# One attention stage, its work put in another order on three engines, and two tiles cut to their natural size

## What is computed

```python
Q = normalize((x @ W_q.T)); K = normalize((x @ W_k.T)); V = x @ W_v.T      # per head
Qn = normalize(einsum('bthd,hde->bthe', Q, W_nudge))
scores = einsum('bqhd,bkhd->bhqk', Qn, K) * SCALE
s = sigmoid(3.0 * einsum('bthd,rd->bthr', K, simple_roots))
cw = prod(s[..., None, :] * bits + (1 - s[..., None, :]) * (1 - bits), -1)  # 16 weights
scores += einsum('bthc,hc->bth', cw, chamber_bonus) of the key             # then causal mask
out = (softmax(scores) @ V).reshape(b, t, 1024) @ W_out.T
```

## Time and profile before

| | |
|---|---|
| median of 3 runs | 1827.04 us (1826.31 to 1828.17) |
| profiled execution, its own time | 1828.17 us |
| span of that execution, first to last instruction | 1826.4 us |
| mean granted TensorE clock | 0.969 of full speed |
| TensorE matmul busy | 1664.5 us, 91% of the span |
| VectorE busy | 1356.9 us, 74% |
| GpSimd busy | 990.9 us, 54% |
| ScalarE busy | 890.1 us, 49% |
| attention layer | from the start to about 833 us |

### The profile page before, as it was taken

One profiled execution on the slowest core, in us unless ns is written; L12 is line 12 of the kernel. 1 busy time (PEld: TensorE's weight loads), 2 busy tenths in 40 slices (PEclk: granted clock), 3 DMA queues, 4 the chain that ended last, 5 costly groups with the idle time before them and its releaser, 6 DMA issues.

```text
span 1826.4 us, 43279 instructions
## 1 busy us (share of the span) xinstructions
PE 1664.5 (91%) x12768; PEld 1245.9 (68%) x12768; DVE 1356.9 (74%) x4113; ACT 890.1 (49%) x2003; POOL 990.9 (54%) x1779
## 2 busy tenths in 40 slices
PE   3999999999999999975999999999999998669996
PEld 2676666676776666754778888888888886435553
DVE  6788888888888887764466777777777775648886
ACT  2665656665556665532444444444444443224443
POOL 5777777777777777752222333333333333227777
PEclk8999999999999999997999999999999999579998
DMA  1011111111111111201011000000000002434441
GB/s 41 10 38 42 52 52 52 52 52 52 44 34 52 52 52 52 81 13 41 12 58 58 30 30 30 30 29 29 29 29 29 29 24 88 155 105 134 130 134 44
DMA packets 78239, 95.76 MB, mean 52 GB/s; under 512 B 7046, under 2 KB 62995, under 8 KB 78160
## 3 DMA queue, kind: packets, MB, share of 16 engines
q1 hardware_dynamic: 70992, 77.91, 13.6%
q0 software_dynamic: 7168, 16.87, 2.6%
HBM read 53.14 MB, written 43.69 MB: 53 GB/s over the span
## 4 chain that ended last, share of the span: by engine, by line
PE 46%; DVE 3%; issue 2%; POOL 2%; ACT 1%; DMA 0%; DVEq 0%; POOLq 0%; SPq 0%; ACTq 0%
PE main L1243 7%; PE main L1245 6%; PE main L1252 6%; PE main L1431 4%; PE main L1269 3%; PE yp L1402 3%; PE xi L1219 3%; PE main L1386 2%; PE main L1389 2%; PE main L1387 2%; PE main L1290 2%; PE route L1445 1%; PE turn L1212 1%; PE xi L1445 1%; PE yp L1453 1%
## 5 line engine op out<-in xcount | busy, mean ns | idle before, releaser
L653 ACT ACTIVATE wgu<-score 128x384 f32<-128x384 f32 x512 | 223.2, 489 | 103.1 <-PE score L476 101.7
L498 PE MATMUL outp<-wgu 128*64 128x256 f32 (+1 forms) x2048 | 197.9, 336 | 29.8 <-POOL wgu L321 28.7
L321 POOL TENSOR_SCALAR_AFFINE_SELECT wgu<-wgu 128x512 f32<-128x512 f32 x256 | 167.1, 653 | 104.4 <-ACT wgu L653 92.1
L1243 PE MATMUL main<-hT_high,h_high 128*128 128x512 f32 x512 | 221.2, 432 | 0.9 <-ACT hT_high L1503 0.9
L1245 PE MATMUL main<-hT_high,h_low 128*128 128x512 f32 x512 | 201.3, 393 | 0.0
L498 PEld LDWEIGHTS outp<-wgu 128*64 128x64 f32 x2048 | 129.4, 138 | 89.5 <-issue 36.4
L1252 PE MATMUL main<-hT_low,h_high 128*128 128x512 f32 x512 | 138.4, 391 | 0.1
L792 DVE TENSOR_TENSOR wgu<-spread,wgu 128x512 f32<-128x512 f32 x128 | 88.5, 691 | 61.0 <-PE spread L520 46.3
L1843 DVE SCALAR_TENSOR_TENSOR th<-th,main 128x512 f32<-128x512 f32 x64 | 43.9, 686 | 114.0 <-ACT th L1570 114.0
L534 PE MATMUL back<-wout,wgu 128*128 128x128 f32 x1024 | 128.1, 279 | 0.0
L1219 PEld LDWEIGHTS xi<-state,wh_sb 128*128 128x128 f32 x512 | 93.8, 196 | 41.0 <-ACT state L1480 23.9
(11 more groups left out here) (272 smaller groups left out, 4299.7 us busy)
## 6 DMA issues: line engine op xcount, KB each, us to landing
sorted_d<-row_buf SPq DMA_DIRECT2D x26, 772.0 KB, 3.7
xg<-sorted_d SPq DMA_DIRECT2D x48, 386.0 KB, 3.1
wgu<-in_gate_up SPq DMA_DIRECT2D x4, 2048.0 KB, 9.4
xa<-in_x SPq DMA_DIRECT2D x32, 128.0 KB, 3.5
xr<-in_x SPq DMA_DIRECT2D x32, 128.0 KB, 3.2
x_d<-x SPq DMA_DIRECT2D x32, 128.0 KB, 1.9
x1c<-x_d SPq DMA_DIRECT2D x16, 256.0 KB, 2.8
x1v<-x_d SPq DMA_DIRECT2D x16, 256.0 KB, 2.8
```

The costliest lines, as they stand in the source:

```text
L321: pool.affine_select(out=blocks, in_=blocks, compare_op=ALU.is_ge, fill=0.0, base=0, pattern=[[0, 4], [1, P]], channel_multiplier=-1).then ...
L498: m = pe.matmul(outp[DV * i:DV * (i + 1), p % 2, k * P:T], val[par][:, k, h, :], weights(h, k), start=(k == 0), stop=(k == 1), tile_positi ...
L653: act.activation(prob[:, h // 2 % (RING // 2), :, h % 2, :], score[h % BANKS][:, 0:SC].rearrange("p (c q) -> p c q", q=P), ACT.Exp).then_i ...
L1243: pe.matmul(main[m % 2][:, :], w[0][:, k, m * P:(m + 1) * P], src[0][:, k, :], start=(k == 0), stop=False)
```

## The change

Three things. (1) `k5` and `cmax` get their natural size: the bonus matmul loads 16 weight columns instead of 128, the `cmax` matmul contracts over 16 rows instead of 128, and two memsets go (N_CONST from 19 to 17). (2) In TensorE's step the pieces stand in another order: the turning of xn comes right behind the first `scores` and ahead of `weighted(z, 3)`; `values` 1, 2 and 3 come earlier, values 3 right behind the bonus; `spread_out(z, 1)` comes ahead of `scores` 4 and `spread_out(z, 2)` ahead of `scores` 5; `scores` 6 comes right behind the `cmax` matmul, with the keys turned behind it; the wait for `rec` is moved ahead of the `outp` matmuls of group 0. (3) ScalarE's and VectorE's steps are put in the matching order. GpSimd's step keeps its order, and so does SyncE's.

```diff
-        k5_wide = sb("k5", [P, P + HEADS, DH + 1])
-        k5 = k5_wide[:, 0:TT * HEADS, :].rearrange("p (i h) c -> p i h c", i=TT)
+        k5 = sb("k5", [P, TT, HEADS, DH + 1])
-        cmax = sb("cmax", [P, T])
+        cmax = sb("cmax", [HEADS, T])
-        N_CONST = 19
+        N_CONST = 17
-                const(pool.memset(k5_wide[:], 0.0))
-                const(pool.memset(cmax[:], 0.0))
@@ weighted, TensorE
                 if g == 0:
                     wait(pe, s["val"], 4 * (b + 1))
+                    wait(pe, s["rec"], b)
...
-                if g == 0:
-                    wait(pe, s["rec"], b)
@@ step, TensorE: the new order
                 scores(b, par, 0)
                 (wait xn, wait qraw; turn xn into front)      # was behind scores 1
                 weighted(z, 1 - par, 3)
                 scores(b, par, 1)
                 values(f, par, 0)
                 (wait xnT; Q and K projection)
                 values(f, par, 1)                             # was behind scores 3
                 scores(b, par, 2)
                 weighted(b, par, 0)
                 spread_out(z, 0)                              # was behind values 1
                 scores(b, par, 3)
                 values(f, par, 2)                             # was behind the bonus
                 (wait bon; turn the bonus, 16 weight columns)
                 values(f, par, 3)                             # was behind the turned qkn
                 spread_out(z, 1)                              # was behind scores 5
                 scores(b, par, 4)
                 weighted(b, par, 1)
                 spread_out(z, 2)                              # was behind the cmax matmul
                 scores(b, par, 5)
                 (wait qkn; turn qkn)
                 (wait cmax; cmax matmul, 16 rows)
                 scores(b, par, 6)                             # was behind the turned keys
                 (wait q5; turn k_aug)                         # was behind the rotation
                 (wait qkT; rotation)
                 spread_out(z, 3)                              # was behind scores 7
                 weighted(b, par, 2)
                 scores(b, par, 7)
                 output(z, par, range(0, 5))
@@ step, ScalarE: moved
+                xnT ahead of copy_out(z, 1 - par, 3)          # was behind weights 2, 3
+                copy_values(f, par, 1) behind sq1             # was behind weights 6, 7
+                copy_values(f, par, 3) behind copy_values 2   # was behind qkT
@@ step, VectorE: moved
+                normalise(z, par, 2) ahead of q5              # was behind q5
+                normalise(z, par, 3) behind k_augT            # was behind the sigmoid and ssg2
```

More of the change, by code:

```diff
@@ L324, in split @@
             def split(value, part, name, n):
-                v = value.rearrange("p i h c -> p (i h c)")
+                v = value[:].rearrange("p i h c -> p (i h c)")
                 parts = [part[:, k].rearrange("p r c -> p (r c)") for k in range(3)]
@@ L437, in step @@
                     wait_apart(pool, s["p_qaT"], f, s["const"])
-                    split(q5[:], q_part, "qsplit", f)
+                    split(q5, q_part, "qsplit", f)
                 mask(b, 6)
@@ L564, in step @@
                 scores(b, par, 0)
-                weighted(z, 1 - par, 3)
-                scores(b, par, 1)
                 if n is not None:
@@ L573, in step @@
                     mm.then_inc(s["p_xnT"], 1)
+                weighted(z, 1 - par, 3)
                 if isinstance(f, int) and f == 0:
@@ L577, in step @@
                     pe.wait_ge(s["wv_split"], 2)
+                scores(b, par, 1)
                 values(f, par, 0)
@@ L586, in step @@
                     mm.then_inc(s["p_qk"], 1)
+                values(f, par, 1)
                 scores(b, par, 2)
                 weighted(b, par, 0)
+                spread_out(z, 0)
                 scores(b, par, 3)
-                values(f, par, 1)
-                spread_out(z, 0)
+                values(f, par, 2)
                 if f is not None:
@@ L597, in step @@
                     for i in range(TT):
-                        mm = pe.matmul(turned[:, i * P:(i + 1) * P], k5_wide[:, i * HEADS:i * HEADS + P, DH], ident[:],
+                        mm = pe.matmul(turned[0:HEADS, i * P:(i + 1) * P], k5[:, i, :, DH], ident[:],
                                        start=True, stop=True)
                     mm.then_inc(s["p_bonT"], 1)
-                values(f, par, 2)
+                values(f, par, 3)
+                spread_out(z, 1)
                 scores(b, par, 4)
                 weighted(b, par, 1)
+                spread_out(z, 2)
                 scores(b, par, 5)
-                spread_out(z, 1)
                 if n is not None:
@@ L618, in step @@
                         mm = pe.matmul(turned[:, T + i * HEADS:T + (i + 1) * HEADS], cmax[:, i * P:(i + 1) * P],
-                                       ident[:, 0:HEADS], start=True, stop=True)
+                                       ident[0:HEADS, 0:HEADS], start=True, stop=True)
                     mm.then_inc(s["p_cmax"], 1)
-                spread_out(z, 2)
+                scores(b, par, 6)
+                if f is not None:
+                    wait(pe, s["q5"], f + 1)
+                    turn_operands(k_aug, "k", f)
                 if n is not None:
@@ L627, in step @@
                     mm.then_inc(s["p_rot"], 1)
[L628 to L632, removed]
+                spread_out(z, 3)
                 weighted(b, par, 2)
                 scores(b, par, 7)
-                spread_out(z, 3)
                 output(z, par, range(0, 5))
@@ L682, in step @@
                     act.activation(xnT[par][:], front[:, 0:T], ACT.Copy).then_inc(s["xnT"], 1)
+                copy_out(z, 1 - par, 3)
+                weights(b, 2, 3)
                 copy_values(f, par, 0)
@@ L688, in step @@
                                    ACT.Square).then_inc(s["sq1"], 1)
+                copy_values(f, par, 1)
                 weights(b, 4, 5)
@@ L695, in step @@
                 weights(b, 6, 7)
-                copy_values(f, par, 1)
                 copy_values(f, par, 2)
+                copy_values(f, par, 3)
                 weights(b, 8, 9)
@@ L840, in step @@
                     wait(dve, s["p_cmax"], f)
-                    dve.tensor_tensor_scan(out=cmax[0:HEADS, :], data0=bonT[:], data1=bonT[:], initial=bonT[:, 0:1],
+                    dve.tensor_tensor_scan(out=cmax[:], data0=bonT[:], data1=bonT[:], initial=bonT[:, 0:1],
                                            op0=ALU.max, op1=ALU.max).then_inc(s["cmax"], 1)
@@ L845, in step @@
                     split_weight(3)
+                normalise(z, par, 2)
+                if last:
                     split_weight(4)
@@ L850, in step @@
                                       -1.0, None, ALU.mult).then_inc(s["q5"], 1)
-                normalise(z, par, 2)
                 if y is not None:
@@ L867, in step @@
                        .then_inc(s["kaT"], 1)
+                normalise(z, par, 3)
                 if last:
@@ L880, in step @@
                     dve.wait_ge(s["ssg2"], n + 1)
-                normalise(z, par, 3)
                 if y is not None:
```

6 lines of the change are left out of this document (1 added, 5 removed).

## The result

| | before | after |
|---|---|---|
| median | 1827.26 us (4 runs, 1826.31 to 1828.17) | 1858.83 us (4 runs, 1858.22 to 1860.25) |
| profiled execution, its own time | 1828.17 us | 1857.88 us |
| span of that execution | 1826.4 us | 1856.1 us |
| mean granted clock | 0.969 | 0.967 |

The ratio is 1.0175, with a 95% interval of 1.0158 to 1.0191: the kernel became slower by 31.6 us. Predicted were 1853 us, between 1826 and 1868.

A forecast was written before the change was run, and what follows sets the result against it. TensorE (91% busy), waiting for GpSimd's mask 3, was taken as the bound. The new loop summed to 25.26 us a step against 24.28: 27 x 0.98 less 1 on 1828.17 gives 1853.7, 1853 for the median; range 1826 to 1868.

The forecast's parts named there:

- The step that decides: Loop from one end of xn to the next through TensorE, GpSimd and VectorE: 25.26 us a step against 24.28.
- X: The moment VectorE finishes xn of the next element, from which the prediction counts the loop.
- X to `spread_out(z, 1)`: From the end of xn to that spread's start, by TensorE's work or VectorE's run to `normalise` 0: 11.12 us average.
- to the end of `scores` 5: TensorE from `spread_out(z, 1)` over `scores` 4, `weighted(b, 1)` and `spread_out(z, 2)` to `scores` 5's end: 3.64 us.
- to mask 5: From the end of `scores` 5 on TensorE to mask 5 on GpSimd: 1.11 us.
- mask 5 to rstd, the wait for q5 gone: GpSimd's stretch from mask 5 to rstd: 7.26 us with a 0.59 wait for q5, 6.67 without it.
- rstd to X: VectorE's yn, x1 and xn behind rstd: 2.72 us.
- wait at xn: TensorE stands for xn of the next element behind `scores` 0, some 0.8 us in every step.
- L520 waits for L792: TensorE's `spread_out(z, 1)` waits for VectorE's `normalise` 0 in every other step of the loop.
- The narrow tiles: Bonus and `cmax` matmuls on TensorE: costed at nothing in the loop; bonus worth up to 0.56 us a step uncovered.
- The wait for `rec`: TensorE's wait at `weighted(b, 0)`: costs nothing, reciprocal ready about 5.2 us after X, matmul starts at 5.5.
- The clock: Rival: TensorE's waits drop its clock once a step, 11 to 32 us on top; 0.11, shared with a longer chain.

The follow-up runs named there:

- e1: Kernel before, with only `spread_out` 1 moved ahead of `scores` 4 and `spread_out` 2 ahead of `scores` 5: 1911.73 us, ratio 1.0461.
- e3: Kernel after, with xn's turning and ScalarE's xnT put back where they were: 1854.98 us, ratio 1.0151.
- e4: Kernel after, with `spread_out` 1 and 2 put back and VectorE's `normalise` 2 behind `q5` again; xn stays early: 1845.52 us, ratio 1.0104.
- e6: Kernel after, with xn's turning, xnT, `spread_out` 1 and 2 and `normalise` 2 all put back: 1838.73 us, ratio 1.0069.
- e7: Kernel before, with GpSimd's mask 3 moved right behind mask 2, ahead of the split of k: 1799.82 us, ratio 0.985.
- e9: Kernel after, with the wide `k5` and the 128-row `cmax` back: 1856.42 us, ratio 1.0162.
- e5: Kernel before, with only `k5` and `cmax` in natural size and the two memsets gone: 1834.71 us, ratio 1.0045.
- e12: Kernel after, with xn's turning and xnT back and the wait for `rec` back between the `outp` and `total` parts: 1868.60 us, ratio 1.0221.
- e8: Kernel after, with GpSimd's mask 3 moved right behind mask 2: 1857.12 us, ratio 1.0168.

## Why the prediction was right, and where it was off

**The step that decides, right.** The loop from xn over `spread_out(z, 1)`, mask 5 and rstd sets the step. Summed: 25.26 us; measured: 25.23 in the step shown, 25.20 on average. e1 shows that asking early for the spreads is enough to close it, without any wait for xn; e3 shows that removing the visible wait of 0.87 us gives 0.07 us a step. e4 and e6 show that undoing parts of the change makes it shorter (24.72 and 24.41) and doesn't open it: in e4 TensorE still waits for xn in each step, in e6 for the reciprocal behind it. In the kernel before it isn't this loop that sets the step but the wait for mask 3, as e7 shows.

**Its terms.**

| term | predicted | measured |
|---|---|---|
| X to `spread_out(z, 1)` | 11.12: TensorE 10.9, VectorE 11.35 in every other step | 11.13 or 11.20, by TensorE in all steps but one |
| to the end of `scores` 5 | 3.64 | 3.54 |
| to mask 5 | 1.11 | 1.10 |
| mask 5 to rstd, the wait for q5 gone | 6.67 | 6.67 |
| rstd to X | 2.72 | 2.72 |
| wait at xn | 0.8 | 0.87 |

The first term is right by two errors, which is luck. VectorE's run was 10.76 us on average and not 11.02, so it didn't decide. TensorE was 0.30 later than summed in the step shown: 0.17 since xn turned takes 0.36 and not 0.19 ahead of `outp`, 0.08 since it starts 0.13 and not 0.05 behind X. V takes 0.89 and 0.90 and not 0.80 ahead of `scores` and the bonus, but the sum had most of that in its 0.37 for `scores` and in the wait ahead of V 3. That L520 waits for L792 in every other step was wrong, then; it did so once. The count of changes of shape was off too: the step has 24 where the prediction counted 22, and 27 with the two narrow pieces.

**The narrow tiles, right where they stand and wrong as a rule.** They cost nothing in the new order (e9). But "the `cmax` matmul still loads 128 columns: nothing" was wrong: it costs 0.28 us a step where TensorE's path is open (e5), by its changes of shape and not by its columns. The bonus matmul saves 0.26 us and not up to 0.56, and 0.10 of that goes again. (No row stood behind the prediction's 0.25 us for it; it takes 0.55.)

**The wait for `rec`, right by a narrow margin.** The reciprocal ends 5.11 to 5.18 us after X, as said, and `weighted(b, 0)` starts 0.63 to 0.68 behind that. Where it does wait for it, in e3 and e6, it starts 0.34 to 0.38 behind, so that some 0.3 us are to spare. It costs nothing only because the wait at xn comes first: in e3 and e6 it is this wait that closes the loop.

**The clock, a rival that didn't come but is real.** No step of the loop after shows a lower clock; TensorE's longest wait there is 0.93 us. In e1 the clock fell 23 times in the loop, behind a wait of 1.96 us, and that is worth about 37 of its 85 us (23 x 1.6); the chain is 27 x (25.66 - 24.28) = 37, and 10.8 lie behind element 28, at the layer's end, not taken apart.

**The sum's other terms.** The loop's part was 26.5 us predicted and 23.5 measured for 27 steps (22.3 + 1.2), because 1.6 us of half clock fell away and the step is 0.92 longer and not 0.98. The start gave nothing where 1 us was taken. The ends of the layer cost 5.9 us, for which the prediction had no term at all: it counted 27 steps and took the last ones as unchanged. The 29.7 us of the two spans are 23.5 + 0.1 + 5.9 and 0.2 in the second block. So the two profiled executions differ by 29.7 us where 25.5 were summed: 5.9 for the ends, 1.1 for the start and 0.2 for the second block, less 3.0 for the loop. The other 2 us by which 1853 falls short are the executions' own spread: the one before lies 1.1 above the median that the prediction started from, the one after 1.0 below its own.

**What bounded the kernel before, right and left unused.** The wait for mask 3 was taken as worth 1.1 us a step at most; one line on GpSimd gives 27 us (e7).

## What to carry to other kernels

A wait that a trace shows is where one engine meets a loop, not what the loop costs: sum the whole loop through every engine from one event to its next occurrence, and ask which other wait stands next in it (here xn, then `rec`, then `normalise` 0, all within 0.5 us a step). When the bound is a wait for another engine, look first at that engine's order, as with mask 3, before reordering the engine that waits. Give the steps that fill and empty a pipeline a term of their own.

## What the runs showed of the hardware

- A change of shape between two pieces on TensorE cost about 0.1 us at each place where it could be seen alone: 0.10 and 0.08 ahead of and behind `cmax` cut to 16 rows, and 0.10 between its first two matmuls (e5). The matmuls themselves didn't change, 0.11 us apart with 128 rows and with 16. Sixteen weight columns instead of 128 brought the four bonus matmuls from 0.22 to 0.11 us apart and the piece from 0.81 to 0.55.
- The granted clock over the same kind of wait: in e1 TensorE waited 1.96 us in each step of 27.28 us, and from 178 us on the clock fell to 1.2 GHz behind it every time, at 1.6 us each, while the first such wait, at 151 us, left it at 2.4 GHz. With waits of 0.93 us and less in each step (after) it stayed at 2.4 GHz; with 0.9 to 1.1 us in each step of e12 it fell three times in the loop; with 0.7 to 1.3 us in each step (before) once.
- The same list of 26 VectorE instructions, from xn to `normalise` 0, took 10.56 (e8) to 11.18 us (e1) on average in different orders of the other engines. Between e3 and e12 the whole difference of 0.34 us is one small instruction, 0.23 us when it starts just ahead of GpSimd's mask and 0.56 when it starts 0.15 us behind its start.
